# Attention with query scores in quarters of 32 queries and 288 keys, set beside the products with the values

## The reference

```python
xn = layernorm(x)
# attention: 16 heads of 16 features, a band of 128 tokens to each side
q, k, v = heads(xn @ w_qkv.T)
s = q @ k.T / 4;  s[|i - j| > 128] = -1e9
attn = (softmax(s) @ v) @ w_proj.T
# feed-forward: a shared expert, and the best 8 of 64 experts by sigmoid
out = x + attn + ffn(xn)
```

## Time and profile before

| | |
|---|---|
| median of 3 runs | 1368.24 us |
| lowest, highest | 1366.77, 1371.7 us |
| span of the profiled execution | 1166.2 us |
| mean granted clock of TensorE over the span | 0.984 |
| first to last key product of attention | 740.4 to 1124.2 us |

### The profile page before, as it was taken

One profiled execution on the slowest core, in us unless ns is written; L12 is line 12 of the kernel. 1 busy time (PEld: TensorE's weight loads), 2 busy tenths in 40 slices (PEclk: granted clock), 3 DMA queues, 4 the chain that ended last, 5 costly groups with the idle time before them and its releaser, 6 DMA issues. The chain is left out here.

```text
span 1166.2 us, 33945 instructions
## 1 busy us (share of the span) xinstructions
PE 1085.4 (93%) x8297; PEld 799.0 (69%) x8298; DVE 767.9 (66%) x2491; ACT 756.1 (65%) x1914; POOL 622.2 (53%) x658
## 2 busy tenths in 40 slices
PE   6989799599999999999999999699999999999999
PEld 3545456399999999999999999355545545455457
DVE  7777779734444444444444457589999998999933
ACT  2555367567777777777777776366666666666653
POOL 0444200176666666666666655466666666666620
PEclk9999899899999999999999999799999999999999
DMA  6888811278888888878877764366665576656413
GB/s 223 216 213 213 240 42 32 94 222 261 247 251 244 252 253 240 250 240 250 253 229 205 206 198 149 101 154 159 154 171 142 142 169 161 152 143 159 122 60 122
DMA packets 143000, 213.84 MB, mean 183 GB/s; under 512 B 19425, under 2 KB 115682, under 8 KB 142946
## 3 DMA queue, kind: packets, MB, share of 16 engines
q0 software_dynamic: 27648, 86.02, 27.6%
q1 hardware_dynamic: 70946, 84.42, 25.9%
q10 hardware_dynamic: 44352, 42.74, 10.6%
HBM read 142.59 MB, written 70.26 MB: 183 GB/s over the span
## 5 line engine op out<-in xcount | busy, mean ns | idle before, releaser
L1076 POOL DMA_INDIRECT xb<-token_rows,idx_ring_x x320 | 303.1, 947 | 179.2 <-issue 140.5
L1104 PE MATMUL psum<-xTe,wb_and_xT_all_or_onorm 128*128 128x128 f32 x2560 | 339.2, 276 | 0.0
L1724 POOL DMA_INDIRECT yg<-expert_rows,idx_ring x256 | 254.2, 993 | 122.5 <-PE psum L1452 45.3
L1227 DVE TENSOR_SCALAR ys<-psum,xb 128x256 f32<-128x256 f32 x320 | 154.9, 484 | 244.7 <-PE psum L1113 243.3
L1104 PEld LDWEIGHTS psum<-xTe,wb_and_xT_all_or_onorm 128*128 128x128 f32 x2560 | 312.4, 192 | 0.1
L1566 ACT ACTIVATE pT<-psum 128x384 f32<-128x384 f32 (+1 forms) x512 | 215.5, 467 | 135.6 <-PE psum L1452 127.7
L1626 DVE CUSTOM_DVE_ANT_0 masked<-psum,mask_q 128x384 f32<-128x384 f32 (+1 forms) x480 | 230.9, 518 | 20.6 <-PE psum L1459 17.2
L1177 ACT COPY wb_and_xT_all_or_onorm<-wb_and_xT_all_or_onorm 128x512 f32 x320 | 197.7, 619 | 18.5 <-SPq L1038 4.8
L1113 PE MATMUL psum<-wb_and_xT_all_or_onorm,aT 128*128 x640 | 191.8, 381 | 0.4 <-issue 0.2
L1163 ACT COPY xTe<-psum 128x256 f32<-128x256 f32 x320 | 119.1, 372 | 102.4 <-PE psum L1094 93.0
L1459 PE MATMUL psum<-qk 96*128 96x384 bf16 (+1 forms) x480 | 154.0, 321 | 29.7 <-DVE nmax L1626 18.4
(11 more groups left out here) (143 smaller groups left out, 1143.0 us busy)
## 6 DMA issues: line engine op xcount, KB each, us to landing
expert_rows<-ys ACTq DMA_DIRECT2D x160, 256.0 KB
wb_and_xT_all_or_onorm<-in_w_exp SPq DMA_DIRECT2D x64, 384.0 KB, 4.2
qk<-q_stacks SPq DMA_DIRECT2D x32, 384.0 KB
q_stacks<-wb_and_xT_all_or_onorm SPq DMA_DIRECT2D x32, 192.0 KB, 2.7
qk<-k_parts SPq DMA_DIRECT2D x32, 192.0 KB
k_parts<-wb_and_xT_all_or_onorm SPq DMA_DIRECT2D x28, 192.0 KB, 3.1
token_rows<-rows SPq DMA_DIRECT2D x8, 640.0 KB, 4.3
xb<-token_rows,idx_ring_x POOLq DMA_INDIRECT x320
```

Of the source, the lines that this page charges most:

```text
L1076: nc.gpsimd.indirect_dma_start(out=xb[:, r, :], out_offset=None, in_=rows_d, in_offset=bass.IndirectOffsetOnAxis(ap=idx_ring[:, q, r:r + 1 ...
L1104: last = nc.tensor.matmul(banks[GU + r % NB][:, part * P:(part + 1) * P], wgu[:, r % NW, h, part * I:(part + 1) * I], xT[:, r % NX, h, :], ...
L1227: nc.vector.tensor_scalar(ys[:, r // 2 % YR, r % 2, :], banks[Y + r % 2][:, 0:D], xb[:, r % XR, bass.ds(e + W_COL, 1)], None, ALU.mult).th ...
L1724: nc.gpsimd.indirect_dma_start(out=yg[:, h, k, :], out_offset=None, in_=y_d, in_offset=bass.IndirectOffsetOnAxis(ap=idx_ring[:, h, k:k + 1 ...
```

## The change

Each query tile of a head is now made by four products of 32 queries. Quarter `z` writes to partitions 32z to 32z + 31 of the bank. In an inner tile a quarter needs only 128 keys to each side of its 32 queries, 288 in all, and its columns begin at key 32z of the window. Edge tiles keep their 256 keys, also in quarters. The maximum of an inner tile reads 288 columns, with a mask of its own, `mask_w`, which three short instructions build at the start of the experts.

In a step the four key scores now come in a row. After them come the query scores of heads 0 and 1, the first part of the products with the values, the query scores of head 2, the second part, and the query scores of head 3.

```diff
+QP = P // 4
+QW = 2 * P + QP
...
+            mask_w = o["mask_w"]
+            nc.vector.tensor_copy(mask_w[:, 0:QP], mask_both[:, 0:QP]).then_inc(o["mask_ready"], 1)
+            nc.vector.memset(mask_w[:, QP:2 * P], 0.0).then_inc(o["mask_ready"], 1)
+            nc.vector.tensor_copy(mask_w[:, 2 * P:QW], mask_both[:, QP:2 * QP]).then_inc(o["mask_ready"], 1)
...
+    def keys_of(i, z):
+        lo, hi = window(i)
+        return (lo * P, hi * P) if hi - lo < 3 else (lo * P + z * QP, lo * P + z * QP + QW)
...
             def scores_q(g, q, i, hh):
-                lo, hi = window(i)
                 reach(pe, s1_free, ahead_entry(g, i, hh) - (RING - 1))
-                nc.tensor.matmul(ring_bank(ahead_entry(like(g), i, hh))[:, 0:(hi - lo) * P], qk[0:KS, q, 0, hh, i * P:(i + 1) * P],
-                                 qk[0:KS, q, 1, hh, lo * P:hi * P], start=True, stop=True).then_inc(s1_ready, 1)
+                bank = ring_bank(ahead_entry(like(g), i, hh))
+                for z in range(4):
+                    a, b = keys_of(i, z)
+                    last = nc.tensor.matmul(bank[z * QP:(z + 1) * QP, 0:b - a],
+                                            qk[0:KS, q, 0, hh, i * P + z * QP:i * P + (z + 1) * QP],
+                                            qk[0:KS, q, 1, hh, a:b], start=True, stop=True)
+                last.then_inc(s1_ready, 1)
...
                 for hh in range(HG):
                     scores_k(g, q, j, hh)
-                    if ahead is not None:
+                if ahead is not None:
+                    for hh in range(2):
                         scores_q(g, qq, i, hh)
                 if exists:
                     before_values(*before)
-                    for part in range(2):
+                for part in range(2):
+                    if exists:
                         values(before[1], part)
+                    if ahead is not None:
+                        scores_q(g, qq, i, 2 + part)
...
-                side = 0 if i > 0 else P
-                nc.vector.tensor_tensor_reduce(masked[:, (i * HG + hh) % 2, 0:(hi - lo) * P],
-                                               ring_bank(place)[:, 0:(hi - lo) * P],
-                                               mask_q[:, side:side + (hi - lo) * P], -1.0, -NEG, ALU.add, ALU.min,
+                if hi - lo < 3:
+                    n, mask = 2 * P, mask_q[:, 0 if i > 0 else P:2 * P if i > 0 else 3 * P]
+                else:
+                    n, mask = QW, mask_w[:, :]
+                nc.vector.tensor_tensor_reduce(masked[:, (i * HG + hh) % 2, 0:n], ring_bank(place)[:, 0:n], mask,
+                                               -1.0, -NEG, ALU.add, ALU.min,
                                                accum_out=nmax[:, hh, i:i + 1]).then_inc(s1_free, 1)
```

More of the change, by code:

```diff
@@ L80 @@
 HIGH = NTOK // 2 - 1
+QP = P // 4
+QW = 2 * P + QP
 MINE = float(1 << 20)
-IOTA = 6 * P + 2 * MB
+IOTA = 6 * P + 2 * QP + 2 * MB
 VALUE = IOTA + NB_ROUTED
@@ L429, in vector @@
         nc.vector.tensor_copy(ident[:, :], consts[:, 0:P]).then_inc(consts_ready, 1)
-        nc.vector.tensor_copy(cb[:, :], consts[:, P:6 * P]).then_inc(consts_ready, 1)
+        nc.vector.tensor_copy(cb[:, :], consts[:, P:6 * P + 2 * QP]).then_inc(consts_ready, 1)
         nc.vector.tensor_copy(iota[:, :], consts[:, IOTA:IOTA + NB_ROUTED])
@@ L737, in table @@
                 chain.done(nc.vector.scalar_tensor_tensor(
-                    junk[:, :], ends, consts[:, 6 * P + c:6 * P + c + 1], one, ALU.is_le, ALU.mult,
+                    junk[:, :], ends, consts[:, 6 * P + 2 * QP + c:6 * P + 2 * QP + c + 1], one, ALU.is_le, ALU.mult,
                     accum_out=cols[:, c:c + 1]))
@@ L942, in opening_tiles @@
     return {
-        "mask_q": sb("mask_q", [P, 3 * P]), "masked": sb("masked", [P, 2, 3 * P]), "nmax": sb("nmax", [P, HG, TT]),
+        "mask_q": sb("mask_q", [P, 3 * P]), "mask_w": sb("mask_w", [P, QW]), "masked": sb("masked", [P, 2, 3 * P]), "nmax": sb("nmax", [P, HG, TT]),
         "nmax_b": [sb(f"nmax_b{k}", [P, HG, 2, b - a], BF16) for k, (a, b) in enumerate(PARTS)],
@@ L999, in experts @@
     ident_b, mask_prev, mask_next = (keep["cb"][:, k * P:(k + 1) * P] for k in (0, 3, 4))
+    mask_both = keep["cb"][:, 5 * P:5 * P + 2 * QP]
     score_bank = banks[PX + 1]
@@ L1273, in _ @@
             nc.vector.tensor_copy(mask_q[:, 2 * P:3 * P], mask_next).then_inc(o["mask_ready"], 1)
-            dve.wait_ge(o["mask_ready"], 3)
+            mask_w = o["mask_w"]
+            nc.vector.tensor_copy(mask_w[:, 0:QP], mask_both[:, 0:QP]).then_inc(o["mask_ready"], 1)
+            nc.vector.memset(mask_w[:, QP:2 * P], 0.0).then_inc(o["mask_ready"], 1)
+            nc.vector.tensor_copy(mask_w[:, 2 * P:QW], mask_both[:, QP:2 * QP]).then_inc(o["mask_ready"], 1)
+            dve.wait_ge(o["mask_ready"], 6)
             for r in range(LEAD - 1):
@@ L1307, in attend @@
     opening = keep["opening"]
-    mask_q, masked, nmax, nmax_b, nmaxT, nrow_in, s1_ready, s1_free, hi_done, nmax_ready, dve_tick, pe_tick = (
-        opening[name] for name in ("mask_q", "masked", "nmax", "nmax_b", "nmaxT", "nrow_in", "s1_ready", "s1_free",
+    mask_q, mask_w, masked, nmax, nmax_b, nmaxT, nrow_in, s1_ready, s1_free, hi_done, nmax_ready, dve_tick, pe_tick = (
+        opening[name] for name in ("mask_q", "mask_w", "masked", "nmax", "nmax_b", "nmaxT", "nrow_in", "s1_ready", "s1_free",
                                    "hi_done", "nmax_ready", "dve_tick", "pe_tick"))
@@ L1824, in build @@
             "w_sh": sb("w_sh", [P, WCOLS]), "wp": sb("wp", [P, 2, D]),
-            "ident": sb("ident", [P, P]), "cb": sb("consts_bf16", [P, 5 * P], BF16),
+            "ident": sb("ident", [P, P]), "cb": sb("consts_bf16", [P, 5 * P + 2 * QP], BF16),
             "v_sb": sb("v_sb", [P, NU, TT, DK]),
@@ L1904, in constants @@
     f[:, 5 * P:6 * P] = np.where(c > r, NEG, 0.0)
-    f[:, 6 * P:6 * P + MB] = r + P * np.arange(MB)[None, :]
-    f[:, 6 * P + MB:6 * P + 2 * MB] = f[:, 6 * P:6 * P + MB] - 1
+    f[:, 6 * P:6 * P + QP] = np.where(r % QP > c[:, 0:QP], NEG, 0.0)
+    f[:, 6 * P + QP:6 * P + 2 * QP] = np.where(c[:, 0:QP] > r % QP, NEG, 0.0)
+    numbers = f[:, 6 * P + 2 * QP:]
+    numbers[:, 0:MB] = r + P * np.arange(MB)[None, :]
+    numbers[:, MB:2 * MB] = numbers[:, 0:MB] - 1
     f[:, IOTA:IOTA + NB_ROUTED] = np.arange(NB_ROUTED)[None, :]
```

## The result

The change took 1440.2 us (median of 4 runs, 1436.47 to 1445.19) against 1368.69 for the kernel before: a ratio of 1.052, with an interval of 1.049 to 1.055. The direction was right, the size was not.

What follows compares the result with a forecast made beforehand. In attention, PE and DVE were both taken as nearly full, each waiting for the other. 0.53 us more in 14 groups (7.4) plus small things made +8 on 1166.2, so 1174; with 202 around the span, 1376, range 1350 to 1390.

Steps and rivals of the forecast that it cites:

- 202 us around the span: Whole run: 202 us of the 1368.24 median lie outside the 1166.2 us span and stay, taking 1174 to 1376.
- Steps 1 to 6: Attention, one group of four heads: step lengths of 2.70, 3.96, 3.34, 2.70, 3.63 and 2.70 us after the change.
- The fourth key product: Inner attention step: it waits for the first exponential, at 1.03 us instead of 0.83; first query set follows at 1.41.
- rivals 3 and 4: Attention quarters: weight loads not hidden, 1410 us, chance 0.08; quarters not running beside each other, above 1530, chance 0.01.
- Step 7: Last step of an attention group: last query set waits for the maximum after step 6's; 2.76 us, was 2.85.
- the walk: Step-by-step sum through an attention group: 24.39 us against 23.84 to 23.87, 0.53 more in each of 14 groups.
- Step 0: First step of an attention group: turn at 1.62 + 0.34 + 0.48 = 2.44, length 2.60 us, was 2.26.
- The first group's guess of 0.4 more: First attention group: its third step waits for rows from memory; its later steps were given 0.4 us more.
- The sum of +8: Whole kernel: 7.4 us from 14 attention groups plus small things, +8 us on a span of 1166.2.
- rival 2: Attention: late starts and shorter maxima nearly cancel, 23.5 to 24.2 us a group, 1368 within a few; chance 0.35.
- DVE's idle time before the first maximum: Sign of being right: in attention steps 4 to 6 this idle time rises above 1 us.
- Rival 1: Attention turns lose their wait and PE's own work sets the group: 21.8 us a group, 1340; chance 0.12.

Runs made afterwards that it cites:

- experiment 6: The change with quarters that take all 384 keys and maxima of 384 columns, against the kernel before, quick chip: 1208.5 us, ratio 1.034.
- 2: The change's order alone, with whole query products and maxima of 384 columns, against the kernel before, quick chip: 1207.3 us, ratio 1.034.
- 15: Kernel before with each 256-column product with the values made as two of 128, 2048 more PE records, quick chip: 1169.9 us, ratio 1.001.
- 17: Second run of the kernel before with its 256-column products with the values split in two, quick chip: 1170.3 us, ratio 1.002.
- experiments 13 and 14: Order alone, then the full change, each against the kernel before on one late chip (before 1379.7 us): 1432.5 us, ratio 1.037; 1457.7 us, ratio 1.055.
- experiment 10: The change with two blocks a step and the maxima of tiles 0 to 4 turned inside step 5, against the kernel before, quick chip: 1158.8 us, ratio 0.992.
- experiment 8: Kernel before in its old order, its maxima reading only 288 of an inner tile's 384 columns, quick chip: 1148.5 us, ratio 0.982.
- first comparison: The change's first measurement against the kernel before, on a late chip: 1440.2 us against 1368.7, ratio 1.052.
- experiment 3: The change's quarters and 288-column maxima in the old order, a query product behind each key product, against the kernel before, quick chip: 1181.7 us, ratio 1.011.

## Why the prediction was wrong, point by point

- **"The median of the runs, 1368.24, holds 202 us around the span, which stay."** This is the step that failed. Only 2 us lie around a span. The 200 us were within the kernel, on a chip where PE's results come late, and I had no row that said what filled them. Nor did they stay: from quick to late chips the kernel before gains 200 to 213 us, the change 253 to 273. That the forecast for the kernel before, 1368, fitted the late runs was only the measured time put back in. A difference between profile and runs of 17% was a sign to distrust the profile as a picture of the runs, and I explained it away. The range should have allowed for an effect that the profile could not show.
- **No rival for the number of PE's records.** The quarters replace 2 records by 8 for each head's query tile, and the sum priced their columns, never their count. On a quick chip that is right: quarters cost 1 us (experiment 6 against 2), 2048 records cost 2 (15, 17). On the late chips the change costs 72 and 78 us instead of 17 to 19, while the order alone costs 53 instead of 38 to 40. So of the 59 us that the change loses more on the late chip of experiments 13 and 14, about 14 come with the order, whose records are as many as before, and about 45 only with the quarters. That the count of records is their cause is argued from the table, not shown. Every kernel that had more records on a late chip had them as quarters, so their narrow form is a rival as good, and the lower clock another. The run that varies the count alone never fell on a late chip. Why results come late there at all stays open.
- **Steps 1 to 6 were right.** Walked 2.70, 3.96, 3.34, 2.70, 3.63, 2.70; measured 2.71, 3.95, 3.33, 2.70, 3.69, 2.71. The fourth key product stands at 1.03 (928.99 to 930.02) and the first set at 1.41 (930.40), as said; eight quarter products and the switch take 0.25 before the values at 930.65:

```profile
930.02 0.34 PE L1484 MATMUL psum<-qk 98*128 98x384 bf16 x1
930.19 0.27 PE L1465 MATMUL psum<-consts_bf 128*128 128x256 bf16 x1
930.40 0.43 PE L1474 MATMUL psum<-qk 96*32 96x288 bf16 x8
...
930.65 0.61 PE L1497 MATMUL psum<-pT,va 128*32 128x256 f32 x8
```

  That excludes rivals 3 and 4, and with them, here, the rule of the Trainium skill's page "TensorE: Matmul & The Clock Gate" (Part 3, packing small matmuls) that weight loads overlap running matmuls only where the row group differs: two sets in 0.25 us, less the switch, are at most 0.125 each. The groups by shape (columns as in the earlier trace rows, 900 to 1120 us of the change on a quick chip) give 452 ns for a maximum of 288 columns, 100 less than before, as expected:

```profile
L1650 DVE CUSTOM_DVE_ANT_0 masked<-psum,mask_w 128x288 f32<-128x288 f32 x212 | 88.6, 452 | 35.6 <-PE psum L1474 35.6
```

  But the same row has 35.6 us of idle time ahead of these maxima. In the kernel before it was 10.0 us ahead of 360 of them. That is 0.17 us for each maximum against 0.03: DVE saves 0.10 in a maximum, and waits 0.14 more.
- **Step 7 was mis-sized: 3.18 instead of 2.76.** The term ended PE's work with the last query set and forgot who waits for the turn of step 5. That turn came 0.9 us later into the step (3.54 for 2.65), its copy and its DMA 0.7, and the DMA's rows are what the next group's first key product needs. The timeline of before had that DMA too, and the walk stopped ahead of it:

```profile
909.57 0.23 PE L1494 MATMUL psum<-consts_bf,nmax_b 128*40 128x128 bf16 x1
...
910.87 0.21 DVE L1645 COPY nmaxT<-psum 40x128 bf16<-40x128 bf16 x1
...
911.11 2.67 SPq L1425 DMA_DIRECT2D qk<-nmaxT  x4
```

  The change on the quick chip:

```profile
942.51 0.22 PE L1511 MATMUL psum<-consts_bf,nmax_b 128*40 128x128 bf16 x1 [0.76 <-DVE nmax L1650]
...
943.64 0.21 DVE L1668 COPY nmaxT<-psum 40x128 bf16<-40x128 bf16 x1
...
943.88 2.65 SPq L1438 DMA_DIRECT2D qk<-nmaxT  x4
```

  From the turned copy's end to that product pass 4.7 us in both kernels (911.08 to 915.80 before, the product in the earlier trace rows, 943.85 to 948.55 now), so the kernel before, whose product shows no wait for it, had next to no slack. Experiment 10, where the turn stands earlier and that wait is gone from the list, bears this out.
- **Step 0 was short by 0.2** (2.79 for 2.60): the second maximum starts 0.40 behind the first, not 0.34, and the turn 0.58 after that, not 0.48.
- On a quick chip these terms make a group 25.1 instead of 24.4. The first group's guess of 0.4 more was wrong the other way (31.6 after 32.3). The sum of +8 measured +17 and +19, which rules out rival 2 as well. One sign of the forecast being right failed: DVE's idle time before the first maximum of steps 4, 5 and 6 was to be above 1 us, and is 0.92, 0.67 and 0.76, although these maxima start 1.94 to 1.95 into the step, as walked.
- **Rival 1 was answered by experiment 8.** The shorter maxima are worth 20 us where the query products come early. The change gives away 39 with its order to gain them.

In sum: on a quick chip the mechanism of the walk was right, and two of its terms were too small by 0.6 us a group. The time of 1440 lies outside the range because of the 202 us that were to stay. That the direction came out right there owes only in part to the walk: 17 to 19 of the 72 us are what it describes.

## What to carry to other kernels

When a product moves later in a step, walk from it to the last one who waits, across engines and through the DMA at the end, and not only to the end of PE's own row. Count instructions as well as columns when a form needs four products for one: on the quick chips 2048 more cost 2 us, on the late one the quarters came with some 45 us of loss, of which the count may be the cause. And where a profile's span and the timed runs differ by more than a few us, say that the profile is not of those runs before building a sum on it.

The best version was that of experiment 10, 0.992 of before on a quick chip. It has the records of the change, and was not run on a late chip, where the change with as many records lost most.

## What the runs showed of the hardware

- Chips differ by 17% for one kernel on one core (1168 against 1368 to 1381 us), with the clock over the whole run at 0.984 against 0.960 to 0.969. On the late ones PE's results reach the engines that wait for them 1 to 2 us after their rows end, again and again in the expert stage and in attention: 1156.7 for rows that end at 1154.73 and 1155.50 (first comparison).
- After a wait DVE starts a maximum 0.21 us after the product's row ends; in a chain of short steps this is as much as the 0.10 saved in each maximum, twice over.
- Four quarter products of 32 columns of weights with 96 rows run beside each other at 0.125 us or less a set of 288 columns at 2.4 GHz, with their weight loads hidden (930.40 to 930.65). Going from full products to this form or back costs 0.10 us (experiment 3).
- A DMA of four issues that brings rows of maxima from one tile to another takes 4.7 us from the end of the copy that it waits for to the start of the product that waits for it (943.85 to 948.55).
